# Fused attention and ternary-weight layer: magnitude sums, sign splits and low weight halves in another order of the preparation

## The chip, the core and the metric

The kernel runs on one core of a Trainium2 chip. The core has five engines with an instruction queue each: TensorE (PE, matrix products), VectorE (DVE), ScalarE (ACT), GpSimd (POOL) and SyncE (SP, which here issues all transfers). Each works its queue in order and waits for the others at counting semaphores. The metric is the time of one execution on the device in microseconds. A profiled execution leaves a trace with the start and the length of every instruction, and the clock granted to PE, 1.00 standing for 2.4 GHz and 0.50 for 1.2 GHz.

## The reference

Eight batches of 512 tokens with 512 channels go through two blocks, each with a layer norm on its output and a residual sum:

```python
x = x + _layernorm(_L0_attn_ref(_layernorm(x), w_attn, b_attn, w_proj, b_proj))
x = x + _layernorm(_L0_ffn_ref(_layernorm(x), w_fc, w_proj))
```

The first is causal attention with 16 heads of 32 channels, queries and keys rotated by an angle that depends on the head alone. The second is a pair of linear layers (512 to 2048 to 512, GELU between) whose weights are made ternary by their own mean magnitude:

```python
gamma = jnp.mean(jnp.abs(w))
w_hat = jnp.sign(jnp.round(w / (gamma + EPS))) * gamma
```

So a weight becomes its sign where its magnitude is above half of (gamma + EPS), else zero, and gamma must be known over the whole matrix before one weight can be decided.

## The kernel before

The program is a chain of iterations `j = -1 .. 8`, written once for every engine in a function `iteration(j, prev, here, nxt, setup)`. Iteration j runs the attention of batch j (`here`), the ternary layers of batch j - 1 (`prev`) and the query, key and value products of batch j + 1 (`nxt`), interleaved by hand through tables such as `QK_AT`, `STEP_MAX` and `LARGE_AT`, which say at which head a piece is put. Iteration -1 is the preparation: no attention yet, only weights, batch 0's products and its row maxima. Iteration 0, called `setup`, has attention but no ternary layers, and finishes the weights.

Precision comes from splitting: a value is kept as a half-precision high part and a half-precision low part (value minus high part). ACT writes the high part ("high"), DVE the low part ("low"), and a product is then three products (high by high, high by low, low by high), each group of 12 matmuls of 512 columns, written by `queries_keys` (L483). The same holds for the value weights (`value_weights`, DVE L1038) and the output weights (`projection_weights`, DVE L1055), each one DVE instruction of 2048 columns behind an ACT copy (`high`, L802).

The products' results lie in three PSUM banks `gen` that are used in turn. Each use has a number in a plan (`FIRST_USES` for the preparation), PE claims a bank when the use three before has been drained, and DVE's low step is what drains it. Three more banks, `score`, are for score tiles and for every second maximum pass. A maximum pass (`max_pass`, PE L543) makes the scores of one head in three banks, and DVE's `maxima` (L1129, L1136) takes row maxima from them, 1.82 us each when nothing holds it. Heads 0 to 15 of batch 0 get theirs in the preparation, before the `shift` transpose (PE L713) that begins the setup iteration; passes with odd heads use `gen`, with even heads `score`.

The ternary weights take these steps for each matrix m (0 for w_fc, 1 for w_down), in four pieces of 2048 columns that lie in `stage` (called hT in the trace, since it shares its memory):

- `magnitudes(m, loaded, i)` on ACT: Sign into t1T or t2T (L904), then Abs in place with a sum over the row (L906)
- `magnitude(m)` on DVE (L1082) adds the four sums, `gamma_total(m)` on PE (L454) adds over the partitions, `thresholds(m)` on DVE makes the threshold
- `large(m, i)` on DVE (L1106) compares the magnitudes with the threshold, `ternary` on POOL (L1518) multiplies signs by the outcome, in four steps a piece; only then may SP load the piece of w_down over the piece of w_fc

`value_bias_projected(c)` on PE (L447) multiplies the value bias with the output weights, four products of single precision, for `projection_bias` on DVE (L1061 to L1066). The x moments on DVE (L1154 to L1167) are for batch 1's layer norm. In the setup iteration PE makes the score tile of head h + 1 ("second tile" is that of head 1), ACT its exponentials, six instructions (L863, L865), DVE the low parts of the probabilities (L1028) which drain the banks for the next tile, and PE the weighted values (L589).

## Time and profile before

| what | us |
|---|---|
| median of 3 executions | 1306.26 |
| lowest and highest | 1306.04, 1308.72 |
| the profiled execution | 1304.86 |
| its span in the trace | 1303.1 |
| PE busy over the span | 1180.7 |
| DVE busy | 990.7 |
| ACT busy | 766.5 |
| POOL busy | 568.7 |

The profiled execution is one of its own, 1.4 us under the median; its span is 1.8 us less than its time. Busy time of PE is the sum of its matmuls, and a matmul at half clock counts twice as long. A time such as 53.65 is counted from the start of the span. In a timeline a row is a run of like instructions: start, length of the run, what it is, and in brackets how long the engine had been idle before and who ended that.

### The profile page before, as it was taken

Reading aid. Unit: us, or ns where it says so; the run is one execution under the profiler, and the core shown is the slowest. Engines: PE = TensorE matmul, PEld = TensorE weight load, DVE = VectorE, ACT = ScalarE, POOL = GpSimd, SP = SyncE. Lnnn points to the kernel's source line nnn. Section 1 sums busy time; section 2 is a strip of 40 time slices with the busy share of each in tenths; the row PEclk is TensorE's granted clock in tenths of the full one; section 3 lists DMA queues with packets and bytes.
Section 4 is the critical chain, followed back from the end, with each engine's and each line's share of the span. In section 5 each row is a group of like instructions: output and inputs, shape, how many; then the busy total and the mean of one; then the engine's idle time right before and its main releaser. Section 6 shows DMA issues by size and latency. Waiting matters only on the chain.

```text
span 1303.1 us, 24731 instructions
## 1 busy us (share of the span) xinstructions
PE 1180.7 (91%) x9300; PEld 646.5 (50%) x9300; DVE 990.7 (76%) x2884; ACT 766.5 (59%) x1410; POOL 568.7 (44%) x634
## 2 busy tenths in 40 slices
PE   6767789999999999999999999999999999988796
PEld 4224444555545554555545554555545554555352
DVE  4587977869787887968887887968887887868532
ACT  4628645676466755666466755666466755567470
POOL 1140603951369213961269213971259312971252
PEclk9897889999999999999999999999999999989899
DMA  8340120012300231012300231012300221001000
GB/s 332 76 151 6 47 80 33 2 29 62 106 1 3 58 94 45 2 25 66 106 1 2 58 87 53 2 26 66 105 1 3 58 67 40 3 2 42 25 1 32
DMA packets 47613, 65.08 MB, mean 50 GB/s; under 512 B 8548, under 2 KB 33156, under 8 KB 46086
## 3 DMA queue, kind: packets, MB, share of 16 engines
q1 hardware_dynamic: 47494, 63.51, 16.5%
q8 instruction: 73, 1.20, 0.4%
q14 instruction: 46, 0.38, 0.1%
HBM read 29.63 MB, written 8.39 MB: 29 GB/s over the span
## 4 chain that ended last, share of the span: by engine, by line
PE 52%; DVE 31%; ACT 11%; issue 3%; POOL 3%; DMA 0%; POOLq 0%; DVEq 0%; ACTq 0%
PE gen L483 19%; PE down L526 17%; DVE score L1136 8%; PE pv L589 4%; DVE hT L1028 4%; PE score L552 4%; DVE probs L1028 2%; PE score L564 2%; PE gen L543 2%; DVE gen L1136 1%; POOL rstd L1480 1%; ACT probs L863 1%; DVE qkn L1231 1%; DVE mx L1136 1%; DVE bn L1167 1%
## 5 line engine op out<-in xcount | busy, mean ns | idle before, releaser
L1480 POOL TENSOR_TENSOR rstd<-veps,mhalf 128x1 f32<-128x1 f32 (+1 forms) x104 | 67.1, 645 | 499.6 <-DVE veps L1215 353.3
L863 ACT ACTIVATE probs<-score 128x512 f16<-128x512 f32 x360 | 189.4, 526 | 118.0 <-PE score L552 118.0
L483 PE MATMUL gen<-x2T,t1T 128*128 128x512 f16 x1024 | 241.6, 381 | 4.0 <-ACT x2T L802 2.5
L526 PE MATMUL down<-t2T,hT 128*128 128x512 f16 x1024 | 235.5, 382 | 3.5 <-DVE xn L1200 3.5
L1028 DVE TENSOR_TENSOR probs<-score,probs 128x512 f16<-128x512 f32 x360 | 199.6, 596 | 51.3 <-ACT score L865 50.9
L865 ACT ACTIVATE score<-score 128x512 f32<-128x512 f32 x360 | 192.1, 534 | 0.0
L483 PE MATMUL gen<-xT,wa 128*128 128x512 f16 x768 | 181.9, 388 | 4.0 <-DVE mx L1136 4.0
L1028 DVE TENSOR_TENSOR hT<-gen,hT 128x512 f16<-128x512 f32 x160 | 108.5, 685 | 63.6 <-ACT gen L822 25.3
L526 PEld LDWEIGHTS down<-t2T,hT 128*128 128x128 f16 x1024 | 96.6, 98 | 110.6 <-DVE xn L1200 4.7
L483 PEld LDWEIGHTS gen<-x2T,t1T 128*128 128x128 f16 x1024 | 95.1, 98 | 108.7 <-ACT x2T L802 5.2
L821 ACT ACTIVATE hT<-gen,gam 128x512 f16<-128x512 f32 x128 | 88.0, 688 | 95.8 <-PE gen L483 95.7
L1136 DVE CUSTOM_DVE_ANT_0 score<-score,mask_rows 128x512 f32<-128x512 f32 (+3 forms) x312 | 143.2, 521 | 0.0
L1509 POOL TENSOR_TENSOR acc<-acc,acc_add 128x512 f32<-128x512 f32 x105 | 133.1, 1268 | 8.2
L1504 POOL TENSOR_TENSOR acc_add<-hT 128x512 f32<-128x512 f16 x105 | 121.3, 1155 | 14.5 <-POOL acc L1509 0.4
L483 PEld LDWEIGHTS gen<-xT,wa 128*128 128x128 f16 x768 | 73.0, 100 | 89.5 <-issue 9.6
L1506 POOL TENSOR_TENSOR acc_add<-acc_add 128x512 f32<-128x512 f32 x105 | 109.3, 1041 | 8.2
L589 PE MATMUL pv<-v_sb,probs 128*128 128x65 f16 x2560 | 102.5, 196 | 9.0 <-DVE oA L1253 9.0
L589 PEld LDWEIGHTS pv<-v_sb,probs 128*128 128x128 f16 x2560 | 96.9, 100 | 16.9 <-DVE probs L1028 13.4
L483 PE MATMUL gen<-wa,xT 128*128 128x512 f16 x384 | 90.9, 386 | 3.7 <-DVE mx L1136 3.7
L1136 DVE CUSTOM_DVE_ANT_0 gen<-gen,mask_rows 128x512 f32<-128x512 f32 x200 | 91.8, 522 | 0.0
L552 PE MATMUL score<-qk 98*128 98x128 f16 x840 | 90.1, 247 | 0.0
L803 ACT ACTIVATE qkn<-gen,qk_bias 128x512 f16<-128x512 f32 x60 | 41.2, 686 | 73.7 <-PE gen L483 73.5
(141 smaller groups left out, 1802.0 us busy)
## 6 DMA issues: line engine op xcount, KB each, us to landing
qk<-qkn SPq DMA_DIRECT2D x360, 64.0 KB, 2.0
xo<-x SPq DMA_DIRECT2D x8, 1024.0 KB, 5.6
hT<-x SPq DMA_DIRECT2D x8, 1024.0 KB, 6.3
out<-xn SPq DMA_DIRECT2D x32, 256.0 KB, 2.2
hT<-w_fc SPq DMA_DIRECT2D x4, 1024.0 KB, 15.9
hT<-w_down SPq DMA_DIRECT2D x4, 1024.0 KB, 5.2
t2T<-w_qk SPq DMA_DIRECT2D x2, 1024.0 KB, 8.7
probs<-w_v SPq DMA_DIRECT2D x1, 1024.0 KB, 11.0
```

The costliest lines, as they stand in the source:

```text
L483: mm = nc.tensor.matmul(bank[:, :], a, b, start=(start and n == 0), stop=(stop and n == len(pairs) - 1))
L526: mm = nc.tensor.matmul(down[:, :], hT[:, half, u, PARTS * tb:PARTS * (tb + 1)], t2T[:, u, :], start=(u == 0 and half == HI), stop=(u == F ...
L552: return nc.tensor.matmul(bank[:, at:at + t1 - t0], qk[0:98, 1, h, PARTS * s:PARTS * (s + 1)], qk[0:98, 0, h, t0:t1], start=start, stop=Tr ...
L589: mm = nc.tensor.matmul(pv[:, VW * tb:VW * (tb + 1)], probs[:, h % 2, half, at:at + PARTS], v_sb[:, s, h, :], start=(s == 0 and half == HI ...
L821: nc.scalar.activation(hT[:, HI, u, :], bank[:, :], ACT.Gelu, scale=gam[:, 0:1])
L863: nc.scalar.activation(probs[:, h % 2, HI, 512 * i:512 * i + n], bank[:, 0:n], ACT.Exp, scale=1.0 / S_UP)
L865: nc.scalar.activation(bank[:, 0:n], bank[:, 0:n], ACT.Exp, scale=1.0 / S_UP).then_inc(exp_full, 1)
L1028: return V.tensor_tensor(out, whole, hi, ALU.subtract)
L1136: op = V.tensor_tensor_reduce(part, part, mask_rows[:, T - n:T], 1.0, -3.0e38, ALU.add, ALU.max, mx[:, TB * u + tb:TB * u + tb + 1])
L1504: P.tensor_tensor(whole[:, :], hT[:, HI, u, :], hT[:, LO, u, :], ALU.add).then_inc(sq_step, 1)
L1506: P.tensor_tensor(whole[:, :], whole[:, :], whole[:, :], ALU.mult).then_inc(sq_step, 1 if u else 2)
L1509: P.tensor_tensor(acc[:, :], acc[:, :], acc_add[:, :], ALU.add).then_inc(sq_step, 1)
```

## The change

Matrix m = 0 gets its steps torn apart. Between the first four query/key products ACT does only Abs with the sum over the row, from `stage` into t1T, which is scratch there. The signs and the magnitudes in place come later as `split(0, i)`, between ACT's value steps, with a new semaphore `magnitude_ready` on which `large(0, i)` waits. For m = 1 the pair stays whole, and the third and fourth pairs go from the start of the setup iteration and head 0 to heads 0 and 1.

ACT's copies of the value and output weights go behind products (2,0) and (2,1), and with them DVE's low halves, that of the output weights out of the setup iteration. The total of the magnitudes goes on PE from behind the third maximum pass to behind the fourth product. The first maximum passes are placed later among the products. The four value-bias products go behind the last four maximum passes, the comparisons `large(0, i)` one into each value turn, those of m = 1 one head later. PE's first wait for `consts` and the casts of DVE goes to where they are read.

```diff
-LARGE_AT = {3: 0, 4: 1, 5: 2, 6: 3}
+GAMMA_AT = 3
+LARGE_AT = {4: 0, 5: 1, 6: 2, 7: 3}
...
-FIRST_USES = (ROT[0:2] + XT[0:2] + ROT[2:4] + XT[2:4] + ROT[4:8] + QK[0:6] + FIRST_MAX[1] + QK[6:8] + FIRST_MAX[3]
+FIRST_USES = (ROT[0:2] + XT[0:2] + ROT[2:4] + XT[2:4] + ROT[4:8] + QK[0:7] + FIRST_MAX[1] + QK[7:8] + FIRST_MAX[3]
...
                     if h == 0:
                         pe.wait_ge(k_rows, 16)
+                        pe.wait_ge(ident_copy, 2)
...
-                    pe.wait_ge(consts, CONSTS)
-                    pe.wait_ge(ident_copy, 2)
                     rotate(0)
                     rotate(1)
+                    pe.wait_ge(consts, CONSTS)
...
-                    for h in range(2 * TB + 4, HEADS):
+                    for c in range(EC):
+                        h = 2 * TB + 4 + c
                         max_pass(h, 1, in_general=(h % 2 == 1))
+                        value_bias_projected(c)
...
-                        if setup and h == 2:
+                        if setup and h == GAMMA_AT:
                             gamma_total(1)
...
-                    flat = t2_flat if m else t1_flat
                     cols = slice(len_piece * i, len_piece * (i + 1))
-                    nc.scalar.activation(flat[:, cols], stage[:, cols], ACT.Sign).then_inc(sign_ready, 1)
-                    act.wait_ge(sign_ready, n + 1)
+                    if m == 0:
+                        nc.scalar.activation(t1_flat[:, cols], stage[:, cols], ACT.Abs, accum_out=gs[:, n:n + 1]
+                                             ).then_inc(g_sums, 1)
+                        return
+                    signs(m, i)
                     nc.scalar.activation(stage[:, cols], stage[:, cols], ACT.Abs, accum_out=gs[:, n:n + 1]
                                          ).then_inc(g_sums, 1)
+
+                def signs(m, i):
+
+                    cols = slice(len_piece * i, len_piece * (i + 1))
+                    flat = t2_flat if m else t1_flat
+                    nc.scalar.activation(flat[:, cols], stage[:, cols], ACT.Sign).then_inc(sign_ready, 1)
+                    act.wait_ge(sign_ready, PIECES * m + i + 1)
+
+                def split(m, i):
+
+                    cols = slice(len_piece * i, len_piece * (i + 1))
+                    signs(m, i)
+                    nc.scalar.activation(stage[:, cols], stage[:, cols], ACT.Abs).then_inc(magnitude_ready, 1)
...
+                    for g in (0, 1):
+                        queries_keys(g, 0)
+                        magnitudes(0, wfc_in, 2 * g)
+                        queries_keys(g, 1)
+                        magnitudes(0, wfc_in, 2 * g + 1)
+                    queries_keys(2, 0)
                     act.wait_ge(wv_in, 16)
                     high(wa[:, HI, :, 2 * E:3 * E], w_v_in, scale=W_UP).then_inc(wv_hi, 1)
...
-                    for tb in range(TB):
-                        values(tb)
+                    split(0, 0)
+                    split(0, 1)
+                    values(0)
+                    split(0, 2)
+                    values(1)
+                    split(0, 3)
+                    values(2)
                     magnitudes(1, wdown_in, 0)
+                    values(3)
                     magnitudes(1, wdown_in, 1)
                     return
...
-                    if setup and h == 0:
-                        magnitudes(1, wdown_in, PIECES - 1)
+                    if setup and h < 2:
+                        magnitudes(1, wdown_in, 2 + h)
...
                         maxima(2 * tb + 4, 1)
-                        if tb < 2:
-                            large(0, 2 + tb)
+                        large(0, tb)
                         v_low(tb)
...
                     halve_maxima()
+                    projection_bias()
                     x_low(0)
                     x_low(1)
-                    projection_bias()
-                    projection_weights()
```

PE in the preparation, from the third product on. Matmuls with gen as output are products, pv is the value-bias product, down the magnitude total. Before:

```order
L483 MATMUL gen<-xT,wa 128x512 x11
L447 MATMUL pv<-x,x2T 33x512 [waits w_ready,p_step,wp_in]
L483 MATMUL gen<-xT,wa 128x512 [waits g_drained]
L483 MATMUL gen<-xT,wa 128x512 x11
L447 MATMUL pv<-x,x2T 33x512 [waits w_ready,p_step,wp_in]
```

Now:

```order
L484 MATMUL gen<-xT,wa 128x512 x11
L484 MATMUL gen<-xT,wa 128x512 [waits g_drained]
L484 MATMUL gen<-xT,wa 128x512 x11
L455 MATMUL down<-gt,ones 128x1 [waits g_step]
L484 MATMUL gen<-xT,wa 128x512 [waits g_drained]
```

The value-bias products are gone from between the products, and the total with its wait on DVE stands behind the fourth. DVE behind the last small step of the x moments (veps). L1231 and L1248 are low halves of query/key products, wait_copy is the first instruction of a maximum step. Before:

```order
L1160 TENSOR_SCALAR veps<-mv 128x4 [waits mv_done0]
L1231 SCALAR_TENSOR_TENSOR x2T<-gen,qk_bias,x2T 128x512 [waits qk_hi]
L1129 COPY wait_copy<-mhalf 128x1 [waits s_full]
```

Now:

```order
L1177 TENSOR_SCALAR veps<-mv 128x4 [waits mv_done0]
L1097 TENSOR_REDUCE gt<-gs 128x1 [waits g_sums]
L1248 SCALAR_TENSOR_TENSOR x2T<-gen,qk_bias,x2T 128x512 [waits qk_hi]
L1104 TENSOR_SCALAR gam<-down 128x1 [waits g_total]
L1107 TENSOR_SCALAR theta<-gam 128x1 [waits g_step]
L1109 TENSOR_TENSOR g_sq<-gam 128x1
L1053 SCALAR_TENSOR_TENSOR wa<-probs,wa 128x4x512 [waits wv_hi,g_step]
L1248 SCALAR_TENSOR_TENSOR x2T<-gen,qk_bias,x2T 128x512 [waits qk_hi]
L1146 COPY wait_copy<-mhalf 128x1 [waits s_full]
```

The sum of sums, the thresholds and the low half of the value weights (wa from probs) have come in between; the low half of the output weights stands behind that maximum step. ACT from the last exponential of head 1's tile on. Before:

```order
L865 ACTIVATE score<-score 128x256
L904 ACTIVATE t2T<-hT 128x2048 [waits g_sums,wdown_in3]
L906 ACTIVATE hT,gs<-hT 128x2048 [waits sign_ready]
L803 ACTIVATE qkn<-gen,qk_bias 128x512 [waits stacked2,g_full]
L863 ACTIVATE probs<-score 128x512 [waits s_full]
```

Now:

```order
L913 ACTIVATE t2T<-hT 128x2048 [waits g_sums,wdown_in2]
L906 ACTIVATE hT,gs<-hT 128x2048 [waits sign_ready]
L801 ACTIVATE qkn<-gen,qk_bias 128x512 [waits stacked2,g_full]
L861 ACTIVATE probs<-score 128x512 [waits s_full]
L863 ACTIVATE score<-score 128x512
L861 ACTIVATE probs<-score 128x512 [waits s_full]
L863 ACTIVATE score<-score 128x512
L861 ACTIVATE probs<-score 128x256 [waits s_full]
L863 ACTIVATE score<-score 128x256
L913 ACTIVATE t2T<-hT 128x2048 [waits g_sums,wdown_in3]
L906 ACTIVATE hT,gs<-hT 128x2048 [waits sign_ready]
L801 ACTIVATE qkn<-gen,qk_bias 128x512 [waits g_full]
```

A pair stands behind the exponentials of head 1 and another behind those of head 2, where there was one.

## Rows read from the trace of the kernel before

**Rows 1.** Busy time by stretches: us, PE, PEld, DVE, ACT, POOL, granted clock, transfers.
```profile
25.00:101.60 76.60, 53.99 (x231) 22.21 (x232) 52.43 (x182) 36.96 (x36) 20.24 (x18) 0.90 0.39 117
101.60:188.70 87.10, 67.21 (x600) 41.29 (x600) 70.42 (x180) 57.55 (x117) 20.19 (x16) 0.79 0.18 47
188.70:1303.10 1114.40, 1047.30 (x8387) 571.82 (x8387) 856.61 (x2498) 661.56 (x1242) 523.01 (x580) 0.99 0.14 38
```

**Rows 2.** Timeline of PE in the preparation: start, length, what [idle before <-who].
```profile
10.67 3.75 PE L632 MATMUL gen<-probs,t2T 128*128 128x128 f32 x16 [10.67 <-DVE mask_b L1034]
...
26.30 7.93 PE L483 MATMUL gen<-xT,wa 128*128 128x512 f16 x36
34.16 1.05 PE L447 MATMUL pv<-x,x2T 128*33 128x512 f32 x2
...
50.83 0.28 PE L543 MATMUL gen<-qk 96*128 96x256 f16 x1 [3.53 <-DVE x2T L1231]
...
53.65 7.91 PE L483 MATMUL gen<-xT,wa 128*128 128x512 f16 x24
...
64.41 1.46 PE L483 MATMUL gen<-wa,xT 128*128 128x512 f16 x6 [1.00 <-DVE mx L1136]
```

**Rows 3.** Timeline of ACT between the first products.
```profile
34.19 1.91 ACT L906 ACTIVATE hT<-hT 128x2048 f32<-128x2048 f32 x1
...
36.10 0.67 ACT L803 ACTIVATE qkn<-gen,qk_bias 128x512 f16<-128x512 f32 x1
36.67 1.90 ACT L904 ACTIVATE t1T<-hT 128x2048 f16<-128x2048 f32 x1
```

**Rows 4.** The tile t2T before 30 us: w_qk's issue, time to landing.
```profile
L342 SPq DMA_DIRECT2D t2T<-w_qk x2: 432/585/738, 1.8 to 2.3; - x2
...
DMA to landing us min/median/max: 7.6/8.7/9.7
```

**Rows 5.** Timeline of DVE: x moments, comparisons with the threshold, output weights' low half.
```profile
41.88 0.68 DVE L1167 BATCH_NORM_STATS2 bn<-xo 128x6 f32<-128x512 f32 x1
...
43.85 0.17 DVE L1160 TENSOR_SCALAR veps<-mv 128x4 f32<-128x4 f32 x1
...
65.27 2.11 DVE L1106 TENSOR_SCALAR hT<-hT,theta 128x2048 f32<-128x2048 f32 x1
...
108.47 2.29 DVE L1055 SCALAR_TENSOR_TENSOR wp<-x,wp 128x2048 f16<-128x2048 f32 x1
...
131.60 1.28 DVE L1106 TENSOR_SCALAR hT<-hT,theta 128x2048 f32<-128x2048 f32 x1
...
136.44 2.18 DVE L1106 TENSOR_SCALAR hT<-hT,theta 128x2048 f32<-128x2048 f32 x1
```

**Rows 6.** Busy time by stretches, cut where the granted clock changed.
```profile
52.00:58.90 6.90, 5.70 (x15) 2.37 (x16) 3.25 (x19) 0.00 (x0) 0.00 (x0) 0.51 0.43 105
...
72.50:76.00 3.50, 3.33 (x9) 1.29 (x10) 1.26 (x8) 0.00 (x0) 3.50 (x4) 0.51 0.92 302
...
96.40:117.00 20.60, 12.53 (x65) 7.85 (x66) 16.41 (x46) 18.33 (x27) 0.00 (x0) 0.50 0.01 3
```

**Rows 7.** Timeline of PE in the setup iteration: score tiles 2, 5, 6 and 8.
```profile
111.42 0.61 PE L564 MATMUL score<-mask_b,identb 128*128 128x512 bf16 x1 [2.25 <-DVE probs L1028]
...
126.96 0.38 PE L564 MATMUL score<-mask_b,identb 128*128 128x512 bf16 x1
...
130.93 0.38 PE L564 MATMUL score<-mask_b,identb 128*128 128x512 bf16 x1
...
139.27 0.61 PE L564 MATMUL score<-mask_b,identb 128*128 128x512 bf16 x1 [2.89 <-DVE probs L1028]
```

**Rows 8.** Timeline of ACT there: exponentials of heads 1 and 3, pair of head 0.
```profile
112.49 0.60 ACT L863 ACTIVATE probs<-score 128x512 f16<-128x512 f32 x1 [1.97 <-PE score L552]
...
115.06 1.91 ACT L904 ACTIVATE t2T<-hT 128x2048 f16<-128x2048 f32 x1
...
122.79 0.59 ACT L863 ACTIVATE probs<-score 128x512 f16<-128x512 f32 x1
```

More of the change, by code:

```diff
@@ L285, in build @@
         v_proj, p_step = sem("v_proj"), sem("p_step")
-        g_sums, g_step, g_total, sign_ready, large_ready, tern_ready = (
-            sem(n) for n in ("g_sums", "g_step", "g_total", "sign_ready", "large_ready", "tern_ready"))
+        g_sums, g_step, g_total, sign_ready, magnitude_ready, large_ready, tern_ready = (
+            sem(n) for n in ("g_sums", "g_step", "g_total", "sign_ready", "magnitude_ready", "large_ready", "tern_ready"))
         c_full, c_ready = sem("c_full"), sem("c_ready")
@@ L929, in iteration @@
                         rotated(n)
+                    for g in (0, 1):
+                        queries_keys(g, 0)
+                        magnitudes(0, wfc_in, 2 * g)
+                        queries_keys(g, 1)
+                        magnitudes(0, wfc_in, 2 * g + 1)
+                    queries_keys(2, 0)
                     act.wait_ge(wv_in, 16)
                     high(wa[:, HI, :, 2 * E:3 * E], w_v_in, scale=W_UP).then_inc(wv_hi, 1)
[L932 to L940 removed]
                     queries_keys(2, 1)
+                    act.wait_ge(wp_in, 16)
+                    high(wp[:, HI, :, :], x1[:, :, :], scale=W_UP).then_inc(wp_hi, 1)
                     queries_keys(3, 0)
                     queries_keys(3, 1)
[L944 to L947 removed]
+                    split(0, 0)
[5 more added lines that the diff above has]
+                    values(2)
                     magnitudes(1, wdown_in, 0)
+                    values(3)
                     magnitudes(1, wdown_in, 1)
@@ L956, in iteration @@
                     normalise(1)
-                    magnitudes(1, wdown_in, 2)
                     x_turned(0)
@@ L1311, in iteration @@
                     bias_ready()
-                    value_weights()
                     qk_low(0, 0)
@@ L1321, in iteration @@
                     x_moments(1, 3)
+                    magnitude(0)
                     qk_low(2, 0)
+                    thresholds(0)
+                    value_weights()
+                    qk_low(2, 1)
                     maxima(0, 1)
-                    qk_low(2, 1)
+                    projection_weights()
+                    qk_low(3, 0)
                     maxima(1, 1, in_general=True)
-                    magnitude(0)
+                    qk_low(3, 1)
                     maxima(2, 1)
-                    thresholds(0)
-                    qk_low(3, 0)
-                    large(0, 0)
-                    qk_low(3, 1)
                     maxima(3, 1, in_general=True)
-                    large(0, 1)
                     for tb in range(TB):
                         maxima(2 * tb + 4, 1)
-                        if tb < 2:
-                            large(0, 2 + tb)
+                        large(0, tb)
                         v_low(tb)
@@ L1376, in iteration @@
                 for h in range(HEADS):
-                    if setup and h == 2:
+                    if setup and h == GAMMA_AT:
                         magnitude(1)
@@ L1394, in iteration @@
                         final_terms(final_at[h])
-                    if setup and h == 2:
+                    if setup and h == GAMMA_AT:
                         thresholds(1)
```

29 lines of the change are left out of this document (6 added, 23 removed).

## Prediction

> **What bounds the kernel now.** I read the busy shares by stage first [rows 1]. From 188.7 us on, TensorE (PE) is busy 1047 of 1114 us at a granted clock of 0.99: the steady batches are bound by PE, and the change touches nothing there. All that it moves lies before: the preparation (25 to 101.6, PE busy 54 of 77 us) and the first batch's heads (101.6 to 188.7, PE busy 67 of 87 us, clock 0.79). So I follow one thing, when PE reaches a mark: first rotation 10.67, first query/key product 26.30, first value product 64.41, transpose of the maxima 101.62, second score tile 111.42, sixth score tile 130.93, first output transpose about 188.7. What that last mark loses or gains, the end does too.
>
> In the preparation PE stops for 3.53 us before 50.83 [rows 2]. Behind it stands ACT: Sign 1.90, Abs 1.91 and the eviction of a product 0.57 (36.10 to 36.67), with the small waits 4.41 us for each product, while PE makes one in 2.60 (36 products in 7.93 us, less the 0.14 by which the last ends late) [rows 2, 3]. That is the stall that the change attacks.
>
> **The change part by part.**
>
> *Start.* PE no longer waits for DVE's two small casts. It still needs the first half of w_qk, issued at 1.8 and landed after 7.6 at the earliest [rows 4], so it starts at 9.5 instead of 10.67. ACT's normalisation stands behind the second rotation and moves with it. **-1.1 us**; first product at 25.2.
>
> *First four products, ACT with sums alone.* ACT now needs 0.57 + 1.91 = 2.48 per product. The form with a sum and a half-precision output isn't in the trace; the nearest rows are Sign with that output, 1.90, and Abs with the sum, 1.91 to the next instruction or 2.01 until its sum is read [rows 3]. I take 1.91; at 2.10 ACT would need 2.67 and cost 0.3 over four. So PE is through at 25.2 + 10.4 = 35.6, and the four value-bias products (0.97 each) are gone from here.
>
> *The new wait.* The total of the magnitudes now stands on PE right behind the fourth product, and all later products are queued behind it. ACT evicts that product until 36.3 and sums until 38.3. DVE has two rows of x moments (2.1 us from 41.88 to the last small step at 43.85 [rows 5]) between its low half of that product (until 37.1) and the sum of sums: 39.3. PE waits **3.7 us** and begins product (2,0) at 39.6.
>
> *The second wait.* PE then makes (2,0), (2,1), a maximum pass (0.6), (3,0), and two banks of the next pass: 39.6 + 7.8 + 1.0 = 48.4. The third bank waits for DVE's low half of (3,0). DVE: low (2,0) until 43.6, thresholds 0.4, ACT's copy of the value weights ready 44.7, their low half 2.2 (2.29 is the row for the same shape [rows 5]) until 46.9, low (2,1) 47.6, maxima 1.82 until 49.4, projection low half 51.6, low (3,0) 52.3. So the two big low halves, said to be early work, lie just there: PE waits **4.0 us**, as long as the wait that was to go. (3,1) needs the first bank of that maximum step (0.82 later) and runs 53.6 to 56.2; ACT, low, maxima and the first bank of the next, 4.3 in all, give the first value product at 60.5.
>
> *Clock.* Before: 64.41. But that contains a stretch of half clock: after the wait of 3.53 us the granted clock was 0.51 from 52.0 to 58.9, and 24 products took 7.91 instead of 5.2 [rows 2, 6]: 2.7 us. At equal clock the new order gains only 1.2, all of it the start. And it has two waits of that length, each with products right behind it: (2,0) and (2,1), +2.7, and (3,1), +2.6. I take both: first value product 65.8, **+1.4**. The Trainium skill (TensorE: Matmul & The Clock Gate, What's actually happening) says that the gate's watch over PE runs freely and doesn't begin anew with the kernel. By that rule the same wait can cost more or less from run to run; a run in which neither wait met it would be 5.3 us shorter. The trace agrees in so far as half clock came in several stretches of unlike length, 3.5 to 20.6 us, where PE had waited [rows 6].
>
> *Value turns.* Four comparisons with the threshold (1.19 in line each while POOL is idle) lie in the turns, 4.8 us. Before, only three lay behind the first value product, but beside POOL: the first took 2.11 where one with POOL idle takes 1.28 [rows 5], so three at 1.2 to 2.0 in line are 3.6 to 6. No gain taken. ACT has 3.85 + 0.6 to do in a turn of 7 us, so its split pairs are hidden; if they weren't, a turn would grow by what is missing. Each turn now has a wait of 2.2 us on PE, so I add one more short half-clock stretch: that of 72.5 to 76 [rows 6] cost at most 1.7, half its length: **+1.2**. The value-bias products (0.97) fit beside DVE's 1.82 per pass in the last four passes. Maxima transposed at 101.62 + 2.6.
>
> *Setup chain.* Before, PE's second score tile waited until 111.42 for DVE, which did the projection's low half (2.29 from 108.47) ahead of the first low probabilities [rows 5, 7]. That is gone, and the bias steps ahead of it lie under the shift's transfer, which wins 0.2 more before ACT's exponentials are late next: 7.3 behind the transpose instead of 9.8, **-2.5**. With the 2.6 lost until then that is nothing won.
>
> *Heads 0 to 4.* ACT takes a pair of 3.85 in head 0 and another in head 1; before, one pair in head 0 and one ahead of the shift's transfer, where ACT had time. Exponentials of head 1 start 1.4 behind the second tile; then ACT runs without a pause: 2.57 + 3.85 + 0.57 + 2.57 + 3.85 + 0.57 = 14.0 until those of head 3. The fifth tile can start 1.8 later: 17.2 behind the second, before 126.96 - 111.42 = 15.5 (exponentials of head 3 at 122.79, 10.3 behind those of head 1 at 112.49; one head's take 2.57, until 115.06) [rows 7, 8]. +1.7. Behind it the magnitude total waits for DVE's output of head 2 and the tile's later banks for the late low halves, 5.5 us until the sixth tile instead of 3.97 (126.96 to 130.93): +1.5. Together **+3.2**.
>
> *Comparisons one head later.* In head 3 the comparison took 1.28 (131.60) with POOL idle; in head 4 already 2.18 beside POOL (136.44) [rows 5]. There PE waits for DVE (2.89 before 139.27 [rows 7]), so a comparison counts in full. Head 3 leaves that series and head 7 joins it: +2.2, less 0.9 because head 4 now has the fast one: **+1.3**. Here head 7's stands ahead of a low half that a maximum pass on PE needs.
>
> *The rest.* Half-clock stretches in the heads before are in the clock of 0.79 [rows 1]. The waits move, their number hardly. I add 0.5, between -2 and +5.
>
> **Sum:** -1.1 - 0.1 + 2.6 (clock, net) + 1.2 - 2.5 + 3.2 + 1.3 + 0.5 = +5.1, say +5.0. The profiled execution took 1304.86 us (span 1303.1), 1.4 less than the median of 1306.26. So 1309.9 for an execution like that one and **1311.3 us** for the median.
>
> **Rivals.**
> 1. *Clock not lost at the two waits.* Both waits come, but the clock stays full behind them: -5.3, so 1306.0. For it: the products behind the first wait are dense, and the clock comes back behind dense work. Against it: both waits are longer than the one of 3.53 us that cost it before.
> 2. *Faster.* The clock holds through the whole preparation, also where it was at half for 20.6 us (96.4 to 117.0 [rows 6]). The place is the last four passes: the four value-bias products add 3.9 us of PE work there. Beside the 5.3 it gives back the 1.2 of the turns and some 2.5 (transposes 1.0, two score tiles 1.3, part of the rest). 1311.3 - 9.0 = 1302.3. It decides for faster as soon as more than 7.6 of the 9.0 come back. Against it: value turns with 2.2 us waits, and DVE alone sets the pace of those passes.
> 3. *More half clock.* PE waits for ACT at the fourth and fifth tiles, 1.3 to 2.1 us each, where it ran closed before. One or two stretches more in the heads, 1.5 to 2.7 each: 1313 to 1316.5.
> 4. *The change doesn't do what it says.* The low halves and the total hold PE no longer than before (the two waits at 1.5 us each): -4.2 in waits and -5.3 in clock, but the heads and comparisons stay: 1301.8. It would need DVE to be ahead by 2.5 us at both places; the durations above leave no room for that.
>
> **How the numbers follow.** Forecast 0.58, rival 1 0.15, rival 2 0.09, rival 3 0.14, rival 4 0.04. The range 1305.0 to 1316.5 takes in the forecast, rivals 1 and 3 and leaves out 0.13 below and some of rival 3's tail. A measurement of this kernel can tell about 0.2%, 2.6 us. Slower means above 1308.9: nearly all of the forecast and rival 3, together 0.67. Within 0.2%: rival 1, the forecast's low end: 0.20. Faster: rivals 2 and 4, 0.13.
>
> **What would show it.** Right: PE waits of 3.5 to 4 us ahead of the total and of the third bank of the second maximum pass; ACT without idle from the exponentials of head 1 to head 3; second score tile 7.3 behind the transpose of the maxima; head 7's comparison at 2.18 and a wait of 2.5 to 3 us of PE's maximum pass behind it. Wrong: a granted clock of 1.0 from 38 to 62 us; a first value product before 62; the sixth score tile less than 21 us behind the second while that one has kept its 2.5.

## The result and the profile after

| | before | changed |
|---|---|---|
| median of 20 runs, us | 1306.09 | 1313.57 |
| lowest and highest | 1305.01, 1308.72 | 1304.66, 1316.10 |
| profiled execution | 1304.86 | 1315.47 |

The ratio is 1.0049 (95% interval 1.0037 to 1.0061): slower by 7.5 us going by the medians, by 6.4 going by this ratio, where 5.0 were forecast. The changed kernel's runs spread over 11.4 us, those of before over 3.7. Three of the 20 lie at 1304.7 to 1305.6, all others at 1310.6 or above. The profiled execution is 1.9 over the median, so what follows shows the change at its dearer side, 10.6 over the profiled execution of before.

Busy time by stretches, cut at the same marks as [rows 1] (us, PE, PEld, DVE, ACT, POOL, granted clock, transfers):

```profile
25.00:108.34 83.34, 60.51 (x228) 24.33 (x229) 52.77 (x182) 42.96 (x39) 19.33 (x18) 0.82 0.37 108
108.34:199.57 91.23, 68.69 (x599) 41.81 (x600) 68.22 (x179) 58.56 (x117) 21.15 (x16) 0.79 0.17 44
199.57:1313.40 1113.83, 1046.01 (x8387) 571.26 (x8387) 857.47 (x2498) 661.62 (x1242) 523.08 (x580) 0.99 0.14 39
```

The steady part takes 1113.8 us where it took 1114.4: all is lost ahead of it. In the first two stretches PE makes the same work (827 matmuls recorded, before 831) and is busy 129.2 us instead of 121.2. A matmul counts longer only at half clock, so some 8 of the 10.9 us by which the first output transpose comes later are PE at half clock, and only some 3 are idle time. The clock of the preparation fell from 0.90 to 0.82.

PE's timeline, the answers to [rows 2] and [rows 7]:

```profile
25.96 10.52 PE L484 MATMUL gen<-xT,wa 128*128 128x512 f16 x48
40.16 0.58 PE L455 MATMUL down<-gt,ones 128*128 128x1 f32 x2 [3.68 <-DVE gt L1097]
40.60 7.67 PE L484 MATMUL gen<-xT,wa 128*128 128x512 f16 x24
...
56.01 0.39 PE L544 MATMUL gen<-qk 96*128 96x256 f16 x1 [4.16 <-DVE xn L1248]
57.31 5.27 PE L484 MATMUL gen<-xT,wa 128*128 128x512 f16 x12 [0.91 <-DVE mx L1153]
...
66.78 2.72 PE L484 MATMUL gen<-wa,xT 128*128 128x512 f16 x6 [2.35 <-DVE mx L1153]
...
108.34 0.30 PE L711 MATMUL gen<-ident,mx 128*128 128x128 f32 x1 [2.42 <-DVE mx L1153]
...
115.70 0.63 PE L566 MATMUL score<-mask_b,identb 128*128 128x512 bf16 x1
...
132.97 0.39 PE L566 MATMUL score<-mask_b,identb 128*128 128x512 bf16 x1 [1.81 <-DVE probs L1043]
...
136.69 4.85 PE L484 MATMUL gen<-xT,wa 128*128 128x512 f16 x12
141.37 0.38 PE L566 MATMUL score<-mask_b,identb 128*128 128x512 bf16 x1
...
162.56 0.39 PE L544 MATMUL gen<-qk 96*128 96x256 f16 x1 [3.27 <-DVE qkn L1248]
```

Four products now run without a pause (10.52 us). Then come the two forecast waits, 3.68 and 4.16 us, each followed by products of twice the usual length: 24 matmuls in 7.67, 12 in 5.27 (full clock: 12 in 2.75). The windows cut where the granted clock changed, as in [rows 6], show six stretches at half clock up to 117 us:

```profile
39.00:45.00 6.00, 4.84 (x13) 2.06 (x14) 1.03 (x5) 0.09 (x2) 1.22 (x2) 0.50 0.41 99
55.60:62.00 6.40, 5.08 (x13) 1.76 (x14) 2.32 (x10) 0.00 (x0) 0.00 (x0) 0.50 0.30 72
66.00:73.00 7.00, 6.22 (x17) 2.45 (x18) 4.18 (x18) 4.76 (x4) 0.00 (x0) 0.52 0.40 95
76.00:79.00 3.00, 3.00 (x10) 1.24 (x9) 0.69 (x5) 1.34 (x1) 2.31 (x3) 0.51 0.00 0
90.00:96.80 6.80, 5.89 (x17) 2.30 (x17) 3.85 (x19) 1.73 (x2) 3.71 (x4) 0.52 0.44 149
109.80:116.90 7.10, 4.36 (x23) 3.42 (x24) 4.55 (x9) 5.12 (x11) 0.00 (x0) 0.53 0.03 7
```

The first two follow the two waits. The next three lie in the value turns, where the kernel before had one of 3.5 us. In the last four maximum passes it is the other way round: the kernel before was at half clock from 96.4 to 117.0 [rows 6], the changed one has 1.00 from 96.8 to 109.8.

The marks, in us from the start of the span, with the shift against the profiled execution of before:

| PE reaches | before | after | shift | forecast |
|---|---|---|---|---|
| first rotation | 10.67 | 9.36 | -1.3 | -1.1 |
| first query/key product | 26.30 | 25.96 | -0.3 | -1.1 |
| first value product | 64.41 | 66.78 | +2.4 | +1.4 |
| transpose of the maxima | 101.62 | 108.34 | +6.7 | +2.6 |
| second score tile | 111.42 | 115.70 | +4.3 | +0.1 |
| sixth score tile | 130.93 | 141.37 | +10.4 | +3.3 |
| first output transpose | 188.69 | 199.57 | +10.9 | +5.1 |

### The profile page after: what moved, and what is told of

Same layout as the page of the kernel before. It is cut to its first block, busy times and chain, and to the rows that moved or that the text cites. A ratio compares the mean times of both kernels' runs of the same rounds, so it can differ in the third digit from the quotient of the medians.

```text
span 1313.4 us, 24743 instructions
## 1 busy us (share of the span) xinstructions
PE 1188.9 (91%) x9300; PEld 650.5 (50%) x9300; DVE 990.0 (75%) x2884; ACT 774.1 (59%) x1414; POOL 568.8 (43%) x634
## 4 chain that ended last, share of the span: by engine, by line
PE 52%; DVE 32%; ACT 10%; issue 3%; POOL 3%; DMA 1%; SPq 0%; POOLq 0%; DVEq 0%; ACTq 0%
PE gen L484 19%; PE down L527 16%; DVE score L1153 8%; PE pv L591 4%; DVE hT L1043 4%; PE score L553 4%; DVE probs L1043 2%; DVE gen L1153 2%; PE gen L544 2%; PE score L566 2%; ACT probs L861 1%; DVE mx L1153 1%; POOL rstd L1494 1%; DVE qkn L1248 1%; DVE bn L1184 1%
## 5 line engine op out<-in xcount | busy, mean ns | idle before, releaser
L484 PE MATMUL gen<-wa,xT 128*128 128x512 f16 x384 | 95.0, 398 | 5.1 <-DVE mx L1153 5.1
```

The costliest lines, as they stand in the source:

```text
L484: mm = nc.tensor.matmul(bank[:, :], a, b, start=(start and n == 0), stop=(stop and n == len(pairs) - 1))
```

## Experiments

The first theory: the order of the change costs 1 to 3 us, and the clock that PE loses behind its new waits the rest. Its rival: the waits themselves and the later exponentials cost it. The control of the clock is a helper that issues small matmuls whose result nobody reads, put where PE would wait ("filled"):

```
+                def fill(n):
+                    for _ in range(n):
+                        nc.tensor.matmul(down[:, 128:512], wa[:, HI, 0, 0:PARTS], wa[:, HI, 1, 0:384],
+                                         start=True, stop=True)
```

Three groups of four runs had each their own runs of the kernel before, with medians 1306.09 (x), 1307.72 (y) and 1305.37 (z). The ratios in the table are to those; a step between groups is uncertain by about 2 us. Each median is that of 5 to 12 runs. A difference "by the ratios" is the difference of two ratios times 1306 us; it can be a microsecond or two off that of the medians, as 6.4 and 7.5 us above.

| run | what | median, us | ratio to before (95%) |
|---|---|---|---|
| x1 | changed, two new waits filled | 1307.96 | 1.0017 (1.0001 to 1.0033) |
| x2 | changed, all waits filled | 1304.32 | 0.9985 (0.9971 to 0.9999) |
| x3 | before, all waits filled | 1301.79 | 0.9961 (0.9947 to 0.9976) |
| x4 | changed, heads undone | 1312.14 | 1.0040 (1.0025 to 1.0055) |
| y1 | changed, total later | 1305.95 | 0.9990 (0.9973 to 1.0007) |
| y2 | changed, output weights' low half undone | 1311.34 | 1.0017 (0.9999 to 1.0034) |
| y3 | x2, heads undone, fills partly as in x3 | 1298.53 | 0.9929 (0.9916 to 0.9942) |
| y4 | total later, heads undone, filled | 1295.82 | 0.9908 (0.9895 to 0.9922) |
| z1 | x1, heads undone | 1304.31 | 0.9992 (0.9981 to 1.0003) |
| z2 | y3, total and comparisons as changed | 1297.86 | 0.9940 (0.9928 to 0.9952) |
| z3 | total later, heads undone, nothing filled | 1304.87 | 0.9979 (0.9965 to 0.9993) |
| z4 | before, start moved | 1304.55 | 0.9994 (0.9982 to 1.0006) |

### x1: the two new waits filled

```
+                    fill(20)
                     gamma_total(0)
...
+                        if nxt and not here and i == 2:
+                            fill(FILL.get(("max", u), 0))
                         if in_general:
                             bank = claim("next max" if here else "first max", 3 * u + i)
```

`FILL` holds 22 for the second maximum pass, so they stand ahead of its third bank.

> The changed kernel, with small matmuls (384 columns, result unused) put on TensorE into its two new waits: 20 ahead of the magnitude total (wait 3.68 us in the trace of after), 22 ahead of the third bank of the second maximum pass (4.16 us). The waits stay, only the clock behind them can change. Theory (half clock behind these two waits costs): products (2,0) and (2,1) take 5.2 instead of 7.67 us, product (3,1) 2.7 instead of 5.27, first value product some 5 us earlier (61.7 instead of 66.8), median 1305 to 1309 instead of 1313.57. Rival (the half clock there is made good again later, by waits that the later stages have anyway): first value product earlier, but median 1312 to 1314. Rival (the clock goes by something else than idle time): nothing changes but some tenths more from the added matmuls.

Measured 1307.96, 5.6 less than the changed kernel. PE's timeline of x1:

```profile
35.56 3.41 PE L538 MATMUL down<-wa 128*128 128x384 f16 x20
39.40 0.38 PE L458 MATMUL down<-gt,ones 128*128 128x1 f32 x2 [0.43 <-DVE gt L1109]
39.64 5.34 PE L487 MATMUL gen<-xT,wa 128*128 128x512 f16 x24
...
48.39 3.74 PE L538 MATMUL down<-wa 128*128 128x384 f16 x22
52.72 0.28 PE L555 MATMUL gen<-qk 96*128 96x256 f16 x1 [0.58 <-DVE xn L1260]
53.91 2.76 PE L487 MATMUL gen<-xT,wa 128*128 128x512 f16 x12 [0.91 <-DVE mx L1165]
...
60.88 2.51 PE L487 MATMUL gen<-wa,xT 128*128 128x512 f16 x6 [2.35 <-DVE mx L1165]
```

DVE still releases the same two steps, so the waits are there, only covered. The 24 matmuls behind the first take 5.34 instead of 7.67, the 12 behind the second 2.76 instead of 5.27. That is the price of the two stretches, 2.33 + 2.51 = 4.8 us, where the prediction had 5.3; the time fell by 5.6 in the medians and by 4.2 by the ratios. The first value product comes 5.9 earlier, but 0.8 of that is there at the first product already (25.20 instead of 25.96). The profiled run (1305.69) is one of the five fastest of 12, which lie at 1305.4 to 1305.7; four lie at 1310.9 to 1314.4. In its trace the value turns, where nothing is filled, were shorter too (38.06 instead of 41.56 us), so it gains more than the median. The rival that the loss would be made good later falls.

### x2 and x3: both kernels with all waits filled

The same helper at most waits over about 1 us in the preparation, at the shift and ahead of score tiles (those of heads 4 to 6 in x2 and 3 to 5 in x3 excepted), in the changed kernel and in the kernel before. The numbers aren't the same in both: at the shift x2 has 10 and x3 14, for instance.

> The changed kernel with the same small matmuls in all waits of TensorE over about 1 us, from the first products to the end of the first batch's heads (4 to 22 in each place, none at heads 4 to 6). Theory (of the 7.5 us that the change costs, most is clock and 1 to 3 are order): granted clock near 1.0 up to the transpose of the maxima, median 1297 to 1303, and only 0 to 3 above the kernel before filled in the same way. Rival (the order itself costs 5 or more, through the waits of 3.7 and 4.2 and the later exponentials): 5 to 8 above the filled kernel before.

> The kernel before with small matmuls in its waits in the same way (18 in the wait of 3.53 us, 12, 12, 8 and 8 in the value turns, 5 behind each of the last four maximum passes, 14 and 14 at the shift, 6 ahead of each score tile but those of heads 3 to 5). It has half clock too, in 52 to 58.9, 72.5 to 76 and 96.4 to 117. Theory: 1298 to 1302 instead of 1306.1, that is 4 to 8 faster, less than the changed kernel gains from it (11 to 16). Rival (the clock is not what parts the two kernels): both gain the same number of us, within 2.

Measured 1304.32 and 1301.79: 9.3 less than unfilled for the changed kernel, 4.3 for the kernel before. x2 missed its forecast (1297 to 1303, a gain of 11 to 16), x3 met its own. 2.5 us stay between the two, in the 0 to 3 that the theory gave; by the ratios it is 3.1 of 6.4, and the two intervals overlap. So a half to two thirds of the loss is clock that filling gives back, and 2.5 to 3 us are left for the order, with what half clock the heads still have (0.91 and 0.94). First x2 by stretches, then x3:

```profile
25.00:98.07 73.07, 64.03 (x328) 30.02 (x327) 52.75 (x182) 42.87 (x39) 19.34 (x18) 1.00 0.41 122
98.07:188.84 90.77, 75.70 (x679) 44.55 (x680) 68.20 (x179) 58.88 (x117) 21.13 (x16) 0.91 0.17 45
```

```profile
25.00:98.24 73.24, 65.15 (x334) 30.42 (x335) 53.15 (x182) 37.10 (x36) 20.24 (x18) 1.00 0.41 122
98.24:184.79 86.55, 72.87 (x680) 42.70 (x680) 70.21 (x180) 57.84 (x117) 20.22 (x16) 0.94 0.19 48
```

With the clock at 1.00 in both, the preparation ends within 0.2 us of the same time (98.07 and 98.24). The change's preparation is no quicker than the old one: PE begins 1.2 earlier, but only 0.3 of that is left at the first product (25.98 and 26.29). All that is left between them lies behind the transpose of the maxima: 90.77 against 86.55. That net holds a gain and a larger loss. The second score tile, first in x2 and then in x3:

```profile
104.88 0.38 PE L577 MATMUL score<-mask_b,identb 128*128 128x512 bf16 x1
...
107.92 0.39 PE L575 MATMUL score<-mask_b,identb 128*128 128x512 bf16 x1 [2.85 <-DVE probs L1046]
```

It comes 6.81 behind the transpose instead of 9.68, so with the clock kept the setup chain gains 2.9 us, and there is no wait for DVE. From that tile to the first output transpose the changed order takes 83.96 instead of 76.87: 7.1 lost.

### x4, y3 and z1: the heads' changes undone

```
-GAMMA_AT = 3
-LARGE_AT = {4: 0, 5: 1, 6: 2, 7: 3}
+GAMMA_AT = 2
+LARGE_AT = {3: 0, 4: 1, 5: 2, 6: 3}
...
                     normalise(1)
+                    magnitudes(1, wdown_in, 2)
                     x_turned(0)
...
-                    if setup and h < 2:
-                        magnitudes(1, wdown_in, 2 + h)
+                    if setup and h == 0:
+                        magnitudes(1, wdown_in, PIECES - 1)
```

> The changed kernel with its changes in the setup iteration undone: third and fourth pair of the second matrix at the start of the iteration and in head 0, magnitude total in head 2, comparisons in heads 3 to 6. Preparation as changed. By the sum of the prediction 3.2 + 1.3 come back: 1309 instead of 1313.57. The profiled run of after lost 6.2 between the second and the sixth score tile (25.67 against 19.51), half clock included, so up to 7: 1306.5. Rival (the heads' loss is only a matter of where half clock falls): 1312 to 1314.

> x2 (changed kernel, waits filled with small matmuls) with the changes in the setup iteration undone as in x4. x4 gave only 1.4 us where 4.5 was expected, with an unsteady clock in both. In the two filled traces the stretch from the second score tile to the first output transpose took 83.96 us (changed) and 76.87 us (before). Theory (the later pairs and comparisons cost 4 to 7 by order, hidden in x4 by where half clock fell): 1297 to 1300.5 instead of 1304.3, also below the filled kernel before (1301.8). Rival (they cost 1 to 2): 1302 to 1304.

> x1 (changed kernel, its two new waits filled, 1307.96) with the changes in the setup iteration undone. With an unsteady clock (x4) undoing them gave 1.4 us, with all waits filled (y3) 5.8. Theory (the order of the heads costs some 5 in itself; in x4 the clock behind the two waits, which swings the time by 5 and more, hid it): 1302 to 1304. Rival (it pays only if the clock is also kept within the heads): 1306 to 1308.

y3 takes most of its fills from x3 (in the value turns, at the shift, and none ahead of the tiles of heads 3 to 5), so it differs from x2 in them too. Undoing the heads' changes gave 1.4 us in the changed kernel itself (x4, where 4.5 to 7 were expected: a miss), 3.7 with the two waits filled (z1 against x1, expected 4 to 6), and 5.8 with all filled (y3 against x2, as expected; 7.3 by the ratios). So the order of the heads does cost, and the steadier the clock the plainer it is (by the ratios the three steps are 1.2, 3.3 and 7.3). Why x4 shows so little isn't settled: its profiled execution was its fastest (1308.04), and from the second score tile to the first output transpose it took 79.01 us against 83.87 in the changed kernel's, which is the expected gain. Four of its seven runs lie at 1312.1 to 1312.6, and none of those has a trace. That they lost the clock elsewhere is likely (their mean granted clock is 0.965 to 0.966, that of the profiled one 0.969), but where isn't shown.

### z2: pairs and comparisons apart

The edit against y3, which also leaves out the six small matmuls ahead of head 6's tile:

```
-GAMMA_AT = 2
-LARGE_AT = {3: 0, 4: 1, 5: 2, 6: 3}
+GAMMA_AT = 3
+LARGE_AT = {4: 0, 5: 1, 6: 2, 7: 3}
```

> y3 (all waits filled, setup iteration as before, 1298.53) but with the magnitude total of head 3 and the comparisons of heads 4 to 7 as changed; only the two pairs on ScalarE are where the kernel before has them. It splits the heads' cost in two. By the prediction's terms (pairs 3.2, comparisons 1.3) it lies 1.3 to 2.2 over y3: 1299.8 to 1300.7. Rival (the comparisons are the larger part, since that of head 7 holds TensorE's maximum pass for 3.27 us where it was 0.82): 2.5 to 4 over y3, 1301 to 1302.5.

Measured 1297.86, 0.7 below y3; by the ratios 1.4 above it. Neither the 1.3 to 2.2 expected nor zero can be told apart by that, but the rival's 2.5 to 4 is out. The traces are nearer to nothing: the first output transpose comes at 182.01 in z2 and 182.48 in y3. PE's timeline of z2 shows the wait at head 7 all the same:

```profile
131.31 0.39 PE L577 MATMUL score<-mask_b,identb 128*128 128x512 bf16 x1 [0.36 <-DVE probs L1063]
...
145.92 0.28 PE L555 MATMUL gen<-qk 96*128 96x256 f16 x1 [2.71 <-DVE qkn L1268]
```

and y3, with the comparisons a head earlier:

```profile
133.56 0.39 PE L577 MATMUL score<-mask_b,identb 128*128 128x512 bf16 x1 [1.91 <-DVE probs L1063]
```

The 2.71 us at head 7 are paid. But the eighth score tile, which in the old order waits behind a slow comparison, comes 2.25 earlier. The move shifts a cost by one head and leaves its sum nearly alone. So the 6.5 us between x2 and z2 (1304.32 and 1297.86, 5.9 by the ratios) are put down to the two pairs on ACT. They hold the half clock behind the pairs' wait, and what the other fills of z2 give isn't parted from them.

### y1: the first wait taken away by order

```
-                    gamma_total(0)
                     queries_keys(2, 0)
                     queries_keys(2, 1)
+                    gamma_total(0)
...
-                    thresholds(0)
                     value_weights()
                     qk_low(2, 1)
                     maxima(0, 1)
+                    thresholds(0)
```

> The changed kernel with the magnitude total on TensorE behind product (2,1) instead of ahead of (2,0), and DVE's thresholds behind its first maximum step. This takes the first new wait (3.68 us) away by order, with no added matmuls. Theory: the sum is ready at 40.1, when TensorE has just made (2,1), so no wait and no half clock behind it; the second wait stays at 4 to 4.6, since DVE's row of low halves sets its end, but 6 us earlier (50 instead of 56.0). First value product at 60.7 instead of 66.8, median 1307 to 1309. Rival (DVE and ACT set the pace, so that the wait only moves to the second place, 7 to 8 us there): first value product under 2 us earlier, median 1312 to 1314.

Measured 1305.95, 7.6 less than the changed kernel and 1 below the theory's 1307 to 1309. PE's timeline of y1:

```profile
24.86 15.70 PE L484 MATMUL gen<-xT,wa 128*128 128x512 f16 x72
...
48.68 0.39 PE L544 MATMUL gen<-qk 96*128 96x256 f16 x1 [4.03 <-DVE xn L1248]
49.98 4.44 PE L484 MATMUL gen<-xT,wa 128*128 128x512 f16 x12 [0.91 <-DVE mx L1153]
...
58.62 1.46 PE L484 MATMUL gen<-wa,xT 128*128 128x512 f16 x6 [2.35 <-DVE mx L1153]
```

Six products in a row, no first wait. The second stays as long as it was (4.03, before 4.16), 7.3 us earlier (1.1 of it from the first product, at 24.86 instead of 25.96), with half clock behind it (4.44 for 12 matmuls). The rival, that the wait only moves, falls. What differs is in DVE's queue: its low half of product (2,0) stands right behind the sum of sums in both. In y1 the product is ready by then:

```profile
38.86 0.15 DVE L1097 TENSOR_REDUCE gt<-gs 128x1 f32<-128x4 f32 x1
38.92 0.74 DVE L1248 SCALAR_TENSOR_TENSOR x2T<-gen,qk_bias,x2T 128x512 f16<-128x512 f32 x1
```

In the changed kernel the product only begins behind that sum, and comes at half clock:

```profile
39.95 0.15 DVE L1097 TENSOR_REDUCE gt<-gs 128x1 f32<-128x4 f32 x1
46.45 0.75 DVE L1248 SCALAR_TENSOR_TENSOR x2T<-gen,qk_bias,x2T 128x512 f16<-128x512 f32 x1 [6.34 <-ACT x2T L801]
```

### y2: the output weights' low half back in the setup iteration

```
-                    projection_weights()
                     qk_low(3, 0)
...
-                    projection_bias()
                     x_low(0)
                     x_low(1)
+                    projection_bias()
+                    projection_weights()
```

> The changed kernel with DVE's low half of the output weights (2.29 us) back in the setup iteration behind the bias steps, where the kernel before had it. Theory: the second new wait goes from 4.16 to 1.9, first value product 2.3 earlier without and 4.9 with the clock kept behind the wait; the second score tile comes 9.6 to 9.8 behind the transpose of the maxima instead of 7.4, which gives 2.4 of it back. Median 1309 to 1313.6. Rival (the move of this step out of the setup iteration was the part of the change that paid, since it sits on that chain in either clock): no clock is saved, 1313.5 to 1316.

Measured 1311.34, inside the theory's range: a gain of 2.2 by the medians, 4.2 by the ratios. The interval ends at 1.0034 where the changed kernel's begins at 1.0037, so it is barely parted from none. PE's timeline of y2:

```profile
54.02 0.28 PE L544 MATMUL gen<-qk 96*128 96x256 f16 x1 [1.96 <-DVE xn L1248]
55.21 4.45 PE L484 MATMUL gen<-xT,wa 128*128 128x512 f16 x12 [0.91 <-DVE mx L1153]
...
63.86 2.72 PE L484 MATMUL gen<-wa,xT 128*128 128x512 f16 x6 [2.35 <-DVE mx L1153]
```

The second wait is 1.96 (expected 1.9) and the first value product 2.9 earlier. So the 2.29 us low half is on PE's path there, nearly one to one (2.20). Half clock came all the same (4.45). The second score tile came 8.6 behind the transpose (103.67 to 112.26) instead of 7.36, so the move out of the setup iteration was worth 1.2 here, not 2.5. PE's transposes ran at half clock in both traces; with the clock kept, x2 against x3 shows 2.9 for the whole chain.

### z4: the earlier start alone

The edit against the kernel before:

```
-                    pe.wait_ge(consts, CONSTS)
-                    pe.wait_ge(ident_copy, 2)
                     rotate(0)
                     rotate(1)
+                    pe.wait_ge(consts, CONSTS)
...
                         pe.wait_ge(k_rows, 16)
+                        pe.wait_ge(ident_copy, 2)
```

> The kernel before with only TensorE's first wait moved, so that it starts at 9.5 instead of 10.67. Theory: all that follows moves by 1.1 to 1.3, 1304.8 to 1305.2. Rival (the clock's pattern shifts against the waits, so that the gain is eaten or doubled): 1303 or 1307, with a wider spread of the runs.

Measured 1304.55, 0.8 less than its runs of before: the forecast 1.1 is within the interval, and so is nothing. The runs spread from 1303.4 to 1309.8, but those of before in the same group from 1304.2 to 1309.8, so the wider spread of the rival isn't shown.

### y4 and z3: a version that beats both

The changed kernel with y1's total (thresholds ahead of the low half of (2,1)), the heads undone as in x4, and the waits filled. z3 has nothing filled and the thresholds where y1 has them, so it isn't quite y4's order. Beside x4's edit and the helper, against the changed kernel:

```
-                    gamma_total(0)
                     queries_keys(2, 0)
                     queries_keys(2, 1)
+                    gamma_total(0)
...
-                    thresholds(0)
                     value_weights()
+                    thresholds(0)
                     qk_low(2, 1)
```

> A version meant to beat both: the changed kernel with the total behind product (2,1), the setup iteration's changes undone, the value-bias products and the early low halves as changed, and the waits filled with small matmuls. If the three effects add (x2 against after -9.3, heads -4 to -7, first wait's 3.7 gone while the second stays): 1290 to 1297. If they overlap (DVE sets the pace once the clock is kept): 1297 to 1300.

> The order of y4 without any added matmul. Theory (the order is better by 3 to 5 than before, but DVE's pace leaves waits and with them half clock): 1300 to 1304, so 4 to 8 over y4 (1295.82). Rival (without a kept clock nothing of it is left): 1305 to 1307.

y4 takes 1295.82 us, 0.9% less than before and 1.4% less than the changed kernel; its five runs lie within 0.9 us. That is in the 1290 to 1297 for effects that add, at its upper end: against y3 the later total gave 2.7 us, not 3.7. z3 takes 1304.87, 9 us more, between what the theory (1300 to 1304) and the rival (1305 to 1307) expected, with runs from 1298.9 to 1305.5. That is 0.5 less than its runs of before by the medians and 2.7 by the ratio, whose interval ends below 1: at most some 0.2% of the order is left without the kept clock. PE's timeline of y4 at the second wait (14 filled matmuls ahead of it, the total at 40.75 without a wait), and its stretches:

```profile
49.01 0.28 PE L555 MATMUL gen<-qk 96*128 96x256 f16 x1 [1.73 <-DVE xn L1267]
```

```profile
25.00:95.05 70.05, 61.62 (x301) 28.04 (x301) 52.05 (x182) 46.60 (x41) 19.33 (x18) 0.98 0.43 127
95.05:177.99 82.94, 70.05 (x680) 41.80 (x680) 68.27 (x179) 55.23 (x114) 20.18 (x16) 0.98 0.19 49
```

The clock of the first heads is 0.98 where it was 0.79 in both kernels. Only here does the change's preparation itself pay: it ends 3.2 ahead of that of x3 (95.05 and 98.24), where those of y3 and z2 end at 98.41 and 98.39. Half clock came behind the second wait even so: the 12 matmuls there take 4.24.

## Why the prediction was right, point by point

The direction, the place and the mechanism were right, and the median lies in the range; two of its terms were too small. (Its "36 products" and "24 products" are matmuls, three products and two; the times worked out from them are right.) By its own steps:

- *Start*: -1.1 forecast, 9.36 instead of 10.67 measured. But only 0.3 of it reached the first product: the rotations between took longer (last section), which the step had not thought of (in x1 and y4 the first product came at 25.2, as forecast).
- *ACT at 2.48 per product*: four products in 10.52 us without a pause, forecast 10.4. Right in what it gives, a little low in size: ACT goes on to read the sum 1.80 behind the start of Abs and to the next product 2.01 behind it (36.52), so it needs 2.59 per product, no more than PE's own 2.60.

```profile
34.51 1.90 ACT L902 ACTIVATE t1T<-hT 128x2048 f16<-128x2048 f32 x1
36.31 0.19 ACT L902 ACTIVATION_READ_ACCUMULATOR t1T<-hT 128x1 f32 x1
```

- *The new wait*: 3.7 forecast, 3.68 measured. *The second wait*: 4.0 and 4.16. Both with the named releaser, and both followed by half clock, +5.3 in the sum; x1 shows 4.8. Rival 1, the same waits with the clock kept, was given 0.15 at 1306.0. Three of the 20 runs lie at 1304.7 to 1305.6, with a mean granted clock of 0.974 where the other 17 have 0.962 to 0.971. The five fastest runs of x1, which has rival 1 by force, have the same times and 0.974 to 0.975. None of the three has a trace, so that they are rival 1 is likely, not shown.
- *Value turns*: this term was mis-sized, +1.2 for one short half-clock stretch. From the first value product to the transpose of the maxima PE took 41.56 us, before 37.21: +4.35. The three stretches of 7.0, 3.0 and 6.8 us stand there. That no gain comes from the comparisons was right: with the clock kept the two orders take 36.50 (x2) and 36.70 (x3).
- *Setup chain*: 7.3 behind the transpose forecast, 7.36 measured. The gain of 2.5 is there against the profiled execution; y2 showed only half of it as the low half's own, x2 against x3 2.9 for the chain with the clock kept.
- *Heads 0 to 4*: the fifth tile 17.2 behind the second forecast, 17.27 measured (115.70 to 132.97). ACT runs as forecast, from the pair of head 0 to the exponentials of head 3 without idle time:

```profile
119.67 1.96 ACT L913 ACTIVATE t2T<-hT 128x2048 f16<-128x2048 f32 x1
...
126.69 1.92 ACT L913 ACTIVATE t2T<-hT 128x2048 f16<-128x2048 f32 x1
...
131.12 0.59 ACT L861 ACTIVATE probs<-score 128x512 f16<-128x512 f32 x1
```

The sixth tile came 8.40 behind the fifth, not 5.5. The product between took 4.85 instead of 2.75 at half clock; in y1, where it kept the clock, the sixth came 5.63 behind the fifth (121.68 to 127.31), so the 5.5 was right for full clock. The term was mis-sized: 3.2 where the marks show 6.1, and z2 against x2 6.5, of which 2.3 are that product (5.04 in x2, 2.75 in z2).
- *Comparisons one head later*: 2.18 for head 7's and a wait of 3.27 behind it, forecast 2.18 and 2.5 to 3:

```profile
159.67 2.18 DVE L1123 TENSOR_SCALAR hT<-hT,theta 128x2048 f32<-128x2048 f32 x1
```

The sum of +1.3 isn't borne out: z2 against y3 gives -0.7 (by ratios +1.4). What the earlier tiles get back was priced at 0.9, for the fast comparison alone; the eighth tile gained 2.25.
- *The rest*: +0.5, between -2 and +5. The clock of the heads stayed at 0.79, over 4 us more. From the sixth tile on the profiled execution lost only 0.5, where this and the comparisons were to cost 1.8.

The marks of the profiled execution came out 5.8 us beyond the forecast: 0.8 at the start, 0.2 up to the first value product, 3.1 in the value turns, 0.1 in the setup chain, 2.9 in the heads, less 1.3 behind them. The two large parts are where half clock came beyond the two places at which it was foreseen. The median lies 2.3 over the forecast; that these are the same parts in smaller measure is argued, since no execution at the median has a trace. Rival 3, more half clock, expected waits of 1.3 to 2.1 us at the fourth and fifth tiles (measured 1.10 and 1.81) and one or two stretches more in the heads. The one at 136.69 is such a stretch, and the median of 1313.57 lies in its 1313 to 1316.5, which had a chance of 0.14. But the larger part, in the value turns, no rival had named, and that the sum stayed within 2.3 of the median is in part luck: the comparisons and the rest took back 1.3 that was not foreseen.

Rival 2, the clock kept through the whole preparation, isn't what happens, but at the place that it named it did: the last four passes ran at 1.00, and the first eight transposes of x took 1.05 us instead of 1.91. It gained nothing there, since the first score tile came 4.21 behind the transpose of the maxima (4.19 before, 4.20 in x2 at full clock). Rival 4, that the two waits would be no longer than before, is out by both rows.

## What to carry to other kernels

When an edit moves waits of a few us on TensorE, price the products behind each wait at both clocks: here half to two thirds of the loss were clock, while at equal clock the new preparation was as long as the old one. A wait at a total, a sum over partitions or another step that nobody needs soon belongs behind work that TensorE can do without it; that alone (y1, with the thresholds moved along) gave back what the change had lost. And a comparison of two orders becomes easier to read once unread matmuls fill the waits of both, because then order and clock mix less.

## What the runs showed of the hardware

- Unread matmuls in waits pay in the kernel before too: 1301.79 against 1306.09, with 5 to 19 of 384 columns at a place, though they add PE work (65.15 against 53.99 us busy in the preparation). Where the clock of the first heads is 0.96 to 0.98 the spread is narrow too (0.9 us in y4, some 2.4 in z2 and y3, 5 or 6 runs each); filling alone doesn't give that, since x2 with 0.91 there has 8.2 us over 12 runs.
- The same wait can be followed by half clock or not. Ahead of the first value product PE waits 2.35 us in the changed kernel, in x1, y1 and y2. In y1 six matmuls behind it took 1.46, in x1 2.51, in the changed kernel and y2 2.72. Half clock also came behind a wait of 1.96 us in y2 (12 matmuls in 4.45). The Trainium skill (TensorE: Matmul & The Clock Gate, What's actually happening) says that the gate's watch runs freely and that where the clock changes therefore varies from run to run. The changed kernel's runs, from 1304.66 to 1316.10 with mean clocks of 0.974 to 0.962, agree; no run here shows one wait of one kernel in two traces.
- An earlier start of PE isn't always passed on. PE began 1.3 earlier in the changed kernel, but the second group of rotations took 2.78 us instead of 2.03 ([rows 2] has the first group alone, 3.75 in both), and the first product came 0.3 earlier. z4 shows the same (first rotation 9.44, second group 2.98, first product 26.24). In x1, y1 and y4 the second group took 2.09 to 2.10 and the first product came at 24.86 to 25.21. The granted clock is recorded as 1.00 from 9 to 25 us in all of these, so the profile's clock doesn't show what slowed it.
